# A decoder layer on one core: SyncE holds its other loads back until the first load has landed

## What is computed

```python
x = x + _L0_attn_ref(_layernorm(x, axis=-1), L0_attn_w_kv_a, L0_attn_q_a_gamma, L0_attn_w_qb, L0_attn_kv_a_gamma, L0_attn_w_kvb, L0_attn_w_o)
x = x + _L0_xattn_ref(_layernorm(x, axis=-1), fside_BxS2xS2_0, ctx_1024)
x = x + _L0_ffn_ref(_layernorm(x, axis=-1), L0_ffn_router_w, L0_ffn_e_bias, L0_ffn_W_gate, L0_ffn_W_up, L0_ffn_W_down, L0_ffn_shared_gate, L0_ffn_shared_up, L0_ffn_shared_down)
```

## Time and profile before

| | us |
|---|---|
| median of 3 executions | 394.71 |
| lowest and highest of them | 391.9 and 395.4 |
| the profiled execution's own time | 394.67 |
| its span | 392.8 |
| TensorE busy (multiplications) | 326.6, 83% of the span |
| VectorE busy | 263.9, 67% |
| ScalarE busy | 173.8, 44% |
| GpSimd busy | 100.5, 26% |
| mean granted clock of TensorE | 0.963 |

### The profile page before, as it was taken

How to read it: one execution, slowest core, us unless ns; L and a number is a source line. 1 busy time by engine, 2 the same in 40 slices (tenths; PEclk the granted TensorE clock), 3 DMA queues, 4 the chain that set the end, 5 groups by cost and what they waited for, 6 DMA issues and landing times.

```text
span 392.8 us, 6578 instructions
## 1 busy us (share of the span) xinstructions
PE 326.6 (83%) x2000; PEld 230.0 (59%) x2000; DVE 263.9 (67%) x1066; ACT 173.8 (44%) x538; POOL 100.5 (26%) x144
## 2 busy tenths in 40 slices
PE   1898999799999789898899899669684897989880
PEld 0555566566866556766566675447573775655660
DVE  2337686775578778788997778795686478334327
ACT  1233566677446755345786435772042230223100
POOL 4112212231030112025233005330016302545500
PEclk9899999999999989999999999999899798999995
DMA  7999592020000000000000000062000400090175
GB/s 261 332 408 361 166 393 112 0 81 2 2 2 0 2 2 2 0 1 26 14 9 5 2 1 2 15 236 81 0 2 3 138 13 0 7 331 18 32 238 195
DMA packets 17895, 34.28 MB, mean 87 GB/s; under 512 B 4780, under 2 KB 9513, under 8 KB 17220
## 3 DMA queue, kind: packets, MB, share of 16 engines
q1 hardware_dynamic: 15556, 32.66, 24.0%
q0 software_dynamic: 2304, 1.20, 1.1%
HBM read 27.10 MB, written 11.99 MB: 100 GB/s over the span
## 4 chain that ended last, share of the span: by engine, by line
PE 52%; DVE 16%; issue 15%; ACT 6%; POOL 5%; DMA 4%; SPq 1%; another core or an unknown queue 0%; POOLq 0%; DVEq 0%; ACTq 0%
PE psum L527 41%; PE psum L536 11%; DVE x_residual L1526 2%; POOL expert_rows L1612 2%; DMA region_a<-token_parts 2%; DVE region_t L1176 1%; DMA x_residual<-in_x_dram 1%; ACT region_t L933 1%; ACT region_r L881 1%; DVE region_t L1184 1%; DVE region_t L1174 1%; POOL rstd L1571 1%; DVE bn_stats L1074 1%; ACT region_t L931 1%; DVE region_t L1165 1%
## 5 line engine op out<-in xcount | busy, mean ns | idle before, releaser
L527 PE MATMUL psum<-region_h,region_b 128*128 128x256 f32 (+1 forms) x320 | 66.4, 343 | 3.4 <-ACT region_b L881 2.2
L527 PE MATMUL psum<-region_c,region_h 128*128 128x512 f32 x128 | 61.6, 606 | 0.5 <-issue 0.5
L931 ACT ACTIVATE region_t<-region_t,neg_max 128x128 f32<-128x128 f32 x64 | 25.6, 399 | 65.4 <-DVE neg_max L1176 65.0
L527 PEld LDWEIGHTS psum<-region_h,region_b 128*128 128x128 f32 x320 | 47.0, 191 | 11.2 <-issue 4.4
L1583 POOL TENSOR_TENSOR q_chunk<-q_chunk,q_rope_tmp 128x256 f32<-128x256 f32 x32 | 23.5, 734 | 110.3 <-DVE q_chunk L1155 110.2
L1612 POOL DMA_INDIRECT expert_rows<-h_moe,slot_scatter x32 | 32.5, 1016 | 25.4 <-issue 14.4
L536 PE MATMUL psum<-consts,region_t 128*128 128x128 f32 x192 | 32.2, 277 | 6.5 <-DVE region_t L1184 3.1
L527 PEld LDWEIGHTS psum<-region_c,region_h 128*128 128x128 f32 x128 | 23.2, 195 | 18.9 <-issue 18.0
L536 PEld LDWEIGHTS psum<-consts,region_t 128*128 128x128 f32 x192 | 23.0, 141 | 17.6 <-issue 12.4
L933 ACT ACTIVATE region_t<-region_t,neg_max 128x256 f32<-128x256 f32 x64 | 31.6, 494 | 0.0
L527 PE MATMUL psum<-w_folded_out,region_g 128*128 128x256 f32 x128 | 29.8, 381 | 0.0
(11 more groups left out here) (189 smaller groups left out, 616.0 us busy)
## 6 DMA issues: line engine op xcount, KB each, us to landing
region_a<-in_experts_dram SPq DMA_DIRECT2D x17, 384.0 KB, 5.9
region_b<-in_experts_dram SPq DMA_DIRECT2D x10, 384.0 KB, 6.1
region_a<-in_fold_dram SPq DMA_DIRECT2D x3, 1152.0 KB, 12.9
token_parts<-region_g SPq DMA_DIRECT2D x12, 256.0 KB, 6.0
region_a<-token_parts SPq DMA_DIRECT2D x6, 512.0 KB, 6.8
region_c<-in_experts_dram SPq DMA_DIRECT2D x5, 384.0 KB, 3.4
expert_rows<-region_g SPq DMA_DIRECT2D x10, 132.5 KB, 11.1
region_h<-expert_rows SPq DMA_DIRECT2D x5, 256.0 KB, 3.8
```

The source lines that it names most:

```text
L527: return nc.tensor.matmul(out_, lhsT, rhs, start=first, stop=last)
L931: nc.scalar.activation(pr[:, 0:P], pr[:, 0:P], ACT.Exp, bias=nmax[:, hn, 0:1], scale=-1.0, accum_out=sums[:, hn, 0:1])
```

## The change

SyncE waits for the semaphore of its first load before it issues the second. Everything behind it in SyncE's list is unchanged and in the same order, and so are all instructions of the other engines; the lines behind the new one have numbers higher by one.

```diff
             sp.dma_start(xres[:, 0:2, :], x[:, 0:2]).then_inc(ld["x0"], 16)
+            sp.wait_ge(ld["x0"], 16)
             sp.dma_start(cst[:], consts[:, 0:NCONST]).then_inc(ld["consts"], 16)
             sp.dma_start(wkva, w_kv_a).then_inc(ld["wkva"], 16)
             sp.dma_start(vec[:], vectors).then_inc(ld["vec"], 16)
```

## The result

| | before | after |
|---|---|---|
| median of 22 executions, us | 394.70 | 392.66 |
| lowest and highest, us | 391.62 and 397.38 | 390.10 and 395.09 |
| ratio, 95% interval | | 0.9946 (0.9924 to 0.9969) |
| span of the profiled execution, us | 392.8 | 391.9 |
| its mean granted clock | 0.963 | 0.965 |

The changed kernel is faster by 0.54%, 2.0 us of the medians, by the interval 1.2 to 3.0 us. The forecast was 0.4 us slower.

What follows compares the result with a forecast made beforehand. The prediction took TensorE's opening, waiting on x and its normalisation, as the bound. x 0.4 us earlier, but consts later, moved the first transpose from 8.56 to 8.93: +0.4 us on 394.67, giving 395.1; range 392.6 to 397.0.

Steps and rivals of the forecast that it cites:

- What bounds the opening: Opening: x lands at 5.31, transposes start at 8.56 us; shifting that shifts the end equally, unless another load turns late.
- Term 1: First load, x: takes 4.2 us instead of 4.59, landing at 4.92, 0.4 us earlier; its chain is ready at 8.17.
- The signs: Chain of waits after: x landed at 4.7 to 5.3, first transpose released by consts at 8.1 to 9.7.
- Term 2: Load of consts behind the wait: takes 3.9 us, lands at 8.9, sets the first transpose at 8.93, +0.4 us.
- Term 3: Load of wkva behind consts: there at 9.8, wanted by TensorE at 10.16; hidden, costs nothing.
- Term 4: Loads behind wkva: all move by about 2.4 us, smallest cover 5.1 us, so they cost nothing.
- The sum: Whole kernel: +0.4 us on the profiled execution's 394.67 us, giving 395.1.
- The rival of the quicker start: Opening: followers caused x's tail; x lands at 3.52, consts at 7.1; -1.5 us, 393.2; chance 0.15.
- Its sign: Chain of waits after: x landing before 4 us would show the quicker start to be right.
- The clock: TensorE after the opening: a shift can lose or add a half-speed stretch, 1.6 us either way; chance 0.15.
- The two rules of the Trainium skill: DMA loads: ring order alone leaves x at 5.31, sum +0.7 us; issuing early and waiting late speaks against the change.

Runs made afterwards that it cites:

- third profile: The changed kernel run unaltered a third time, against the kernel before; ratio 0.9989 (0.9954 to 1.0023).

## Why the prediction was wrong

- **What bounds the opening** was right: x, its chain of 3.25 us, then the transposes, and whatever shifts them shifts what follows. The changed kernel's lead of 2.94 us over the first profile before at 84 us is still 2.79 at 247 us.
- **Term 1, the landing of x, failed, and with it the sign.** It was taken at 4.2 us and measured 3.08 to 3.12. The counts of packets were read rightly: 106 of 128 were reckoned to have started by 3.75 us, and 105 had. The step that failed is the next one, that the 4.6 us came from a slow start of the program and not from the followers, because bandwidth was free. At the same start of the program, with nothing behind it, x took 3.1 us, and the time grew with what followed: 3.25, 3.72, 4.45, 4.6 us. Nor was it only a tail of 22 packets, as the counts at 2.75 us show. (The signs named x at 4.7 to 5.3 us, where the forecast's own ends make it 4.52 to 5.32.) The load of 256 KB that took 2.8 us with four followers at 308.97 us was the wrong witness against that; why it is immune is open.
- **Term 2, consts,** was taken at 3.9 us and measured 3.15 to 3.25 in the three profiles of the changed kernel. The lower bound, 3.5, was already too high. It had been built from 384 KB in 3.2 to 3.4 us with 0.15 us for the larger size; the 444 KB took no longer than the 384 KB. This miss alone would have turned the sign too: with x landing at 4.92 as forecast, consts would have come at 4.98 + 3.25 = 8.23 us, ahead of the 8.56 of before. With consts at 3.9 and x as measured the transposes would have started at some 7.8.
- **Term 3, wkva,** held: it landed at 4.24 + 3.7 = 7.9 us, and TensorE wanted it at 8.41.
- **Term 4** held in its first half and not in its second. The last rope piece landed at 6.37 + 10.3 = 16.7 us, 1.8 us later than before (2.4 were reckoned). But its cover was counted to a use at 20.39 us. That use moved too, by the earlier start and by the missing stretch, to 17.48, and of 5.5 us of cover 0.8 were left. In the third profile it was gone. Cover must be counted between the new landing and the new use.
- **The sum** was +0.4 us; the opening gives -1.4. The rival of the quicker start had it: 3.52 for x (3.84 measured), consts in 3.5 (3.25), -1.5 us for the transposes (-1.41). Its sign, x landing before 4 us, is the one that came true. It had a chance of 0.15, too little beside three rows that all pointed at a load into an empty queue taking about 3 us.
- **The clock** as a rival was right in kind and size: 1.6 us either way. The range held the median by 0.06 us, and only because the 1.6 us of a half-speed stretch had been taken off its lower end. That was luck: the opening was not as described.
- **The two rules of the Trainium skill** (DMA: Bandwidth & Descriptors). Descriptors in ring order on each engine, from its section on queues, rings and completion order, gave x at 5.31 when read as "x has nothing to gain". The measured 3.84 goes against that reading: being first in each ring did not make the whole load land undisturbed. Issuing early and waiting late, from the page's rules for kernel authors, is the rule that this case goes against: the loads issued 2.7 us later brought the first transpose 1.4 us forward. The fit of that page of the Trainium skill, given for DMAs issued from GpSimd, makes 3.0 us for consts as an estimate, and came nearer to the 3.25 than the 3.9 taken from rows.

## What to carry to other kernels

Where a kernel opens with one load on which everything hangs, what is issued behind it is not free, even while the engines move far less than they can: here the first load took longer with the kilobytes that followed. That was seen at the start of the program only; a load of the same size later on the earlier trace rows took 2.8 us with four behind it. Issuing the rest 2 us after the first load was enough here, waiting for the load itself was not needed, and what is behind must then be checked against uses that have moved earlier too. And before a stretch of slow clock in one profile is put into a sum, the unaltered kernel should be profiled once more.

## What the runs showed of the hardware

- 256 KB as the only load in flight at the start of the program land in 3.1 us; with 144, 444 and 908 KB issued right behind, in 3.25, 3.7 and 4.5 us. Of its 128 packets 81 to 83 had started by 2.75 us alone, and 65 to 70 with everything behind it, though at most four packets of the others had started by then.
- A load of 444 KB into a drained queue, with others behind it, landed in 3.15 to 3.5 us, as fast as 384 KB (3.2 to 3.4).
- One kernel, profiled twice, had a half-speed stretch of TensorE of 3.4 us at 15.9 us in one execution and full clock in the other; the first query multiplication moved by 1.66 us.
- The granted clock is given as 1.00 over the first microseconds in all these profiles, while the records of the same multiplication take 4.61 us cold and 2.39 us after a warm-up. The durations tell the level there, and the column does not.
